# Scores of a second cross-attention from high and low halves in the round format, with keys kept in DRAM

## The chip, the cores and the metric

The kernel runs on one NeuronCore of a Trainium2 chip. The metric is the device time of one execution in microseconds; less is better. The core has TensorE (PE) for matmuls, VectorE (DVE), ScalarE (ACT) and GpSimd (POOL) for everything else, and SyncE (SP), which issues most of the DMAs here. The engines run their own instruction streams and meet only at semaphores.

## The reference, cut to what matters

Two layers of a perceiver-like network act on x (2 sequences of 64 tokens, 256 wide) with a context of 2 x 1024 rows of 512. Each layer is a cross-attention, a second mixing block and a mixture of eight experts. The change concerns the cross-attention of the second layer, in which each of 16 heads has 16 dimensions, the keys and values of the 1024 context rows are slices of the context itself, and those of the 64 tokens of the own sequence are projected:

```python
qkv = (x @ w_qkv.T).reshape(B, N, 3, H, D).transpose(2, 0, 3, 1, 4)
kv = context.reshape(B, N_c, 2, H, D).transpose(2, 0, 3, 1, 4)
k = jnp.concatenate([extra_k, k], axis=2)
attn = jnp.einsum('bhnd,bhmd->bhnm', q * scale, k)
attn = jax.nn.softmax(attn, axis=-1)
out = jnp.einsum('bhnm,bhmd->bhnd', attn, v)
return out @ w_proj.T + b_proj
```

## The kernel before

The program is written out engine by engine in one block; no planner orders it. It runs: first cross-attention, self-attention, first experts (units `f1b` to `f2e7`), second cross-attention, a state-space block with memory, second experts (`m1e0` to `m2e7`), store.

**Two number formats.** A matmul on plain float32 operands leaves two records per instruction in the trace. One whose operands have the type float32r (the round format) leaves one. For exactness a product in the round format is made from halves: `hi` is the value rounded to the format, `lo` is what is left, and a product of two split operands takes three matmuls (`TERMS`). The first cross-attention (`sim`, L1552; `attend`, L1596) and the experts (L1755, L1836) work so. The split halves of the context lie in `CXT` (turned, keys along the free axis) and `CXN` during the first cross-attention.

**Second cross-attention.** It is done in 16 rows of work, r = 0 to 15; row r is head pair j = r // 2 of sequence b = r % 2, with 128 query rows (2 heads x 64 tokens). For each r:

- `sim1(r)` (PE, L1890) makes 128 x 1024 scores in two plain float32 matmuls of 512 columns, one for each half `kh` of the keys. Each contracts over 32 partitions, and the two lie in different row groups of the array (`at = 64 * (j % 2) + 32 * kh`). `QZ` holds the queries, masked by head.
- DVE takes the maximum (L1244), and -max (L1254).
- ACT takes the exponential of the 1024 scores (L837) and of the 64 own scores (L841), which lie in `SELF`.
- `turn1(r - 2)` (PE, L1935) turns the 1152 probabilities in three groups c of three 128 x 128 transposes; ACT copies groups 0 and 2 out (L828), DVE group 1 (L1262).
- `attend1(r - 3)` (PE, L1953) multiplies them with the values, 9 matmuls in four column groups.

PE's order is sim1(r), turn1(r - 2), attend1(r - 3). `sim1(r)` waits for the exponential of row r - 2, whose scores used the same PSUM pair. Ahead of the loop PE projects the queries and the own keys (L1877, eight matmuls each, with weights that ACT laid out as `WDUP`, L800), makes sim1(0) and sim1(1), the own scores of both sequences for all pairs (`own_scores`, L1904), ten filler matmuls (`stay_warm`, L1475) and the own values (L1918). DVE adds `b_proj`, halves `D` and builds `hmask` just ahead of `QZ` (L1195 to L1201). `PV` collects the products and is copied out on DVE every four rows (L1230); `spread_sums` is L1217.

**POOL during this stage** splits the weights of `m1e0` and `m1e1` (four pieces of 1024 columns, L554 and L558), then splits bias rows (L609, L612) and scales a weight (L618). DVE's `spread_sums(0)` waits for the end of the bias rows, since both use `work`.

**Weights and the DMA queue.** Weights come in units of 1 MB, issued in a fixed order (`PLAN`) on SP's queue. A unit is loaded into a place once the unit that was there has been released. After the first cross-attention a cycle of NA + NB = 8 places is used (5 in `arena`, 3 in `ctxmem`); the other units of `ctxmem` hold `KEYS` (keys of the second cross-attention, 2 MB from the transposed context, L522) and `ctxN` (values, L523), which are loaded behind `f1e2`, and are filled with expert weights once the second cross-attention is through.

## Time and profile before

| | us |
|---|---|
| median of 3 runs | 467.27 (466.98 to 467.71) |
| the profiled execution | 467.19 |
| its span, first to last instruction | 465.4 |
| PE busy | 447.5 (96%) |
| DVE busy | 258.5 (56%) |
| ACT busy | 240.4 (52%) |
| POOL busy | 125.3 (27%) |

The span is what the trace shows; the profiled execution's own time is 1.8 us more. PE is busy for nearly all of the span, but its records are pipelined: a record of a matmul is longer than the step from one matmul to the next, so that steps between starts say more than durations. The granted TensorE clock is 1.0 over the whole span.

### The profile page before, as it was taken

How to read it: one execution, taken by the hardware profiler on the slowest of the kernel's cores; microseconds unless marked ns; L12 is line 12 of the kernel's file. 1: busy time of each engine (PE TensorE's matmuls, PEld its weight loads, DVE VectorE, ACT ScalarE, POOL GpSimd, SP SyncE). 2: the span in 40 equal slices, each digit the busy share in tenths (PEclk: the TensorE clock that was granted, in tenths of full speed). 3: DMA queues.
4: the chain of work that ended last, by engine and by line, in shares of the span. 5: the costliest groups of instructions: out<-in, count | busy, mean ns of one | idle time of the engine just before them, and what ended most of it. 6: DMA issues, size and time to landing. Idle time of an engine off the chain costs nothing.

```text
span 465.4 us, 8504 instructions
## 1 busy us (share of the span) xinstructions
PE 447.5 (96%) x3500; PEld 384.2 (83%) x3500; DVE 258.5 (56%) x455; ACT 240.4 (52%) x439; POOL 125.3 (27%) x113
## 2 busy tenths in 40 slices
PE   8999999999999999999987999999999999999997
PEld 7887989999897989999976677998666779778797
DVE  2656223245426233232045788978667765569996
ACT  2577334264445333252113778772888774347872
POOL 1120000002000500000021267988900000019795
PEclk9999999999999999999999999999999999999999
DMA  7925400005200020049990489891000039264000
GB/s 283 409 99 195 180 2 1 0 1 174 100 0 1 13 90 1 1 156 328 235 367 1 162 339 393 301 361 80 3 1 1 2 130 411 94 270 182 0 1 13
DMA packets 13191, 62.65 MB, mean 135 GB/s; under 512 B 1365, under 2 KB 3813, under 8 KB 7392
## 3 DMA queue, kind: packets, MB, share of 16 engines
q1 hardware_dynamic: 11072, 54.31, 31.7%
q0 software_dynamic: 2080, 7.80, 4.6%
q8 instruction: 28, 0.46, 0.4%
q14 instruction: 11, 0.09, 0.1%
HBM read 61.97 MB, written 0.13 MB: 133 GB/s over the span
## 4 chain that ended last, share of the span: by engine, by line
PE 78%; DVE 6%; ACT 6%; POOL 6%; issue 3%; DMA 1%; SPq 0%; DVEq 0%; ACTq 0%; POOLq 0%
PE W L1596 20%; PE W L1552 15%; PE W L1755 8%; POOL w_lo L558 5%; PE W L1836 4%; PE W L1890 4%; PE W L1935 3%; PE W L1569 3%; PE W L1953 2%; PE W L1618 2%; PE W L1475 2%; PE W L1856 1%; POOL small L567 1%; PE W L1877 1%; PE W L1659 1%
## 5 line engine op out<-in xcount | busy, mean ns | idle before, releaser
L1596 PE MATMUL W<-probs_turned_hi,ctx_split_hi 128*128 128x256 f32 x256 | 72.9, 285 | 2.5 <-issue 2.5
L1596 PE MATMUL W<-probs_turned_hi,ctx_split_lo 128*128 128x256 f32 x256 | 72.5, 283 | 0.0
L1596 PE MATMUL W<-probs_turned_lo,ctx_split_hi 128*128 128x256 f32 x256 | 72.4, 283 | 0.0
L1030 DVE TENSOR_TENSOR probs_turned_lo<-W,probs_turned_hi 128x512 fp32r<-128x512 f32 x32 | 20.6, 686 | 64.9 <-ACT probs_turned_hi L699 64.9
L1596 PEld LDWEIGHTS W<-probs_turned_hi,ctx_split_hi 128*128 128x128 f32 x256 | 49.1, 192 | 3.7 <-issue 3.3
L567 POOL TENSOR_TENSOR small<-small,const 128x1 f32<-128x1 f32 (+2 forms) x10 | 7.0, 699 | 164.5 <-DVE small L1103 75.3
L1596 PEld LDWEIGHTS W<-probs_turned_lo,ctx_split_hi 128*128 128x128 f32 x256 | 49.1, 192 | 0.2
L1596 PEld LDWEIGHTS W<-probs_turned_hi,ctx_split_lo 128*128 128x128 f32 x256 | 49.1, 192 | 0.0
L558 POOL TENSOR_TENSOR w_lo<-arena,w_hi 128x320 fp32r<-128x320 f32 x30 | 42.1, 1424 | 25.9 <-ACT w_hi L640 25.6
L718 ACT ACTIVATE pbuf<-W,small 128x1024 f32<-128x1024 f32 x16 | 17.9, 1117 | 59.5 <-DVE small L1050 59.5
L558 POOL TENSOR_TENSOR w_lo<-ctxmem,w_hi 128x320 fp32r<-128x320 f32 (+1 forms) x30 | 47.2, 1600 | 4.2 <-ACT w_hi L640 3.9
L993 DVE TENSOR_TENSOR w_lo<-arena,w_hi 128x704 fp32r<-128x704 f32 (+1 forms) x34 | 43.2, 1304 | 5.8 <-ACT w_hi L640 5.4
L1836 PE MATMUL W<-w_hi,acts 128*128 128x256 f32 x240 | 44.2, 286 | 0.0
L1552 PE MATMUL W<-ctx_turned_hi,q_keys_hi 128*128 128x512 f32 x128 | 41.1, 402 | 0.5 <-DVE q_keys_lo L1023 0.5
L640 ACT CAST w_hi<-arena 128x1024 fp32r<-128x1024 f32 x34 | 35.5, 1049 | 8.5 <-PE W L1755 4.1
L1552 PE MATMUL W<-ctx_turned_lo,q_keys_hi 128*128 128x512 f32 x128 | 39.7, 391 | 0.0
L1552 PE MATMUL W<-ctx_turned_hi,q_keys_lo 128*128 128x512 f32 x128 | 39.5, 390 | 0.0
L1836 PEld LDWEIGHTS W<-w_hi,acts 128*128 128x128 f32 x240 | 38.3, 191 | 0.1
L710 ACT COPY scr<-W 128x256 f32<-128x256 f32 x32 | 11.8, 368 | 48.9 <-PE W L1596 48.9
L993 DVE TENSOR_TENSOR w_lo<-ctxmem,w_hi 128x704 fp32r<-128x704 f32 x26 | 33.8, 1341 | 2.0 <-ACT w_hi L640 1.6
L1836 PE MATMUL W<-w_lo,acts 128*128 128x256 f32 x120 | 33.9, 282 | 0.0
L1042 DVE TENSOR_REDUCE small<-W 128x1 f32<-128x1024 f32 x16 | 19.6, 1223 | 25.5 <-PE W L1552 25.5
(403 smaller groups left out, 921.9 us busy)
## 6 DMA issues: line engine op xcount, KB each, us to landing
arena<-units_dram SPq DMA_DIRECT2D x22, 1024.0 KB, 6.2
ctxmem<-units_dram SPq DMA_DIRECT2D x16, 1024.0 KB, 7.8
fixed<-units_dram SPq DMA_DIRECT2D x6, 1024.0 KB, 6.4
pbuf<-ctx_dram POOLq DMA_DIRECT2D x4, 512.0 KB, 6.3
ctxmem<-ctxT_dram SPq DMA_DIRECT2D x8, 256.0 KB, 14.1
ctxmem<-ctx_dram SPq DMA_DIRECT2D x2, 1024.0 KB, 18.6
scr<-ctx_dram POOLq DMA_DIRECT2D x3, 512.0 KB, 4.1
vecs<-vectors_dram POOLq DMA_DIRECT2D x1, 1040.0 KB, 7.6
```

The costliest lines, as they stand in the source:

```text
L558: pool.tensor_tensor(w_slot(1, p)[:, lo:hi], half_in(p)[:, lo:hi], f32(w_slot(0, p)[:, lo:hi]), ALU.subtract).then_inc(ev("lo_by_gpsimd"), 1)
L640: act.copy(w_slot(0, p), half_in(p)).then_inc(ev(hi_done(p)[0]), 1)
L718: act.activation(probs0[:, r % 2, :], W[r % 2][:, :], ACT.Exp, bias=negm[:, r:r + 1], accum_out=stat[:, r, 1:2]).then_inc(ev("exp_done"), 1)
L993: dve.tensor_tensor(w_slot(1, p)[:, lo:hi], half_in(p)[:, lo:hi], f32(w_slot(0, p)[:, lo:hi]), ALU.subtract).then_inc(ev("lo_by_vector"), 1)
L1030: dve.tensor_tensor(PT[1][at], bank(4 + c).rearrange("p (t m) -> p t m", t=4), f32(PT[0][at]), ALU.subtract).then_inc(ev("pl_sb"), 1)
L1042: step(dve.tensor_reduce(mx[:, r % 2:r % 2 + 1], W[r % 2][:, :], AX_X, ALU.max))
L1552: mm = pe.matmul(W[r % 2][:, kh * 512:(kh + 1) * 512], QP[a][:, c, j, :], CXT[z][:, c, kh * 512:(kh + 1) * 512], start=(c == 0 and n == 0) ...
L1569: mm = pe.transpose(bank(4 + c)[:, t * P:(t + 1) * P], probs0[:, r % 2, (4 * c + t) * P:(4 * c + t + 1) * P], ident)
L1596: mm = pe.matmul(ps, CXN[a][:, t, c * P:(c + 1) * P], PT[z][:, t, :], start=(t == 0 and n == 0), stop=(t == KEYT - 1 and n == 2))
L1755: mm = pe.matmul(bank(4 + hf), XS[a][:, e, k, :], w_slot(z, p)[:, hf * 512:(hf + 1) * 512], start=u == "m1e0" and k == 0 and n == 0, stop= ...
L1836: mm = pe.matmul(bank(n % (E + 1) % 4)[:, 0:DIM], UTS[a][:, t, :], w_slot(z, p)[:, (t % 4) * DIM:(t % 4 + 1) * DIM], start=(t == 0 and i = ...
L1890: mm = pe.matmul(W[r % 2][:, kh * 512:(kh + 1) * 512], QZ[at:at + 32, j // 2, b].rearrange("p h q -> p (h q)"), KEYS[at:at + 32, b, j // 2 ...
```

## The change

It rebuilds the score products of the second cross-attention in the round format.

- **Keys.** The key half of `CXT`, already split into hi and lo for the first cross-attention, is stored to a DRAM buffer `kept_keys` (4 MB in four DMAs on SP's queue), and loaded back later as `KS`, 4 MB in eight DMAs, with hi in partitions 64 kh to 64 kh + 31 and lo in the 32 behind.
- **Queries.** They are projected four times over (`WDUPQ`), so that each 32 dimensions of a pair stand in all four groups of 32 partitions, then masked and split: hi (`QSH`) for pairs 0 to 3 by ACT, for pairs 4 to 7 by POOL from a copy (`QRAW`) that DVE makes; lo (`QSL`) by DVE.
- **sim1(r)** becomes four matmuls of 512 columns in the round format, each over 64 partitions: q hi and q lo, each with both key halves. One matmul over 64 partitions adds q times key hi and q times key lo.
- **Own scores** take 4, 12 and 16 matmuls in the round format at three points (pair 0, pairs 1 to 3, and pairs 4 to 7 within the loop at r = 7), all into PSUM bank 5, which `turn1` uses too. `turn1(6)` waits for DVE to have copied them out.
- **Moved.** `b_proj` to r = 3 of the loop; `D`, `hmask` and two new small steps to r = 1 of the first cross-attention. DVE's wait for the bias rows moves from r = 12 to r = 7.
- **Places.** `KS` takes four units of `ctxmem` where `KEYS` took two, so the cycle of places has 6 instead of 8, and six instead of four units are filled behind the second cross-attention, four of them as soon as all scores are made.

The diff, cut to its core:

```diff
-NR, NA, NB, NC = 4, 5, 3, 4
...
+PARTS_OF = [(kh, part) for kh in range(2) for part in range(2)]
...
-        put(units[freed + n], NR + NA + NB + n, after="xat")
+        put(units[freed + n], NR + NA + NB + n)
+        plan[-1][2].append(("sim1_done" if n < 4 else "pv1_ps", ROWT))
...
+        kept = nc.dram_tensor("kept_keys", (B, 2, DIM, NCTX), F32, kind="Internal").ap()
...
-        KEYS = cut(ctxmem, 0, B, 4, NCTX // 2)
-        ctxN = cut(ctxmem, B * KT * NCTX, B, KEYT, DIM)
+        KS = cut(ctxsplit, 0, B, PAIRS, NCTX // 2)
+        ctxN = cut(ctxmem, 4 * UNIT, B, KEYT, DIM)
...
+            def store_keys(b):
+                sync.wait_ge(ev("ctx_lo"), 8 if b == 0 else 10)
+                for part in range(2):
+                    sync.dma_start(kept[b, part].rearrange("(c p) k -> p c k", p=P), f32(CXT[part][:, 0:KT, :]))\
+                        .then_inc(ev("keys_kept"), 16)
             for n in range(3, len(PLAN)):
                 load(n)
+                if PLAN[n][0] == "wv1":
+                    store_keys(0)
+                if PLAN[n][0] == "att":
+                    store_keys(1)
...
+                    sync.wait_ge(ev("keys_kept"), 2 * B * 16)
                     for b in range(B):
-                        for jp, kh in ROWS_OF:
-                            at = 64 * jp + 32 * kh
-                            src = ctxT_in[b, 0:DIM, kh * 512:(kh + 1) * 512].rearrange("(m j p) k -> j p m k", j=2, p=32)
-                            sync.dma_start(KEYS[at:at + 32, b], src[jp]).then_inc(ev("ctxT_in"), 16)
+                        for kh, part in PARTS_OF:
+                            at = 64 * kh + 32 * part
+                            src = kept[b, part, :, kh * 512:(kh + 1) * 512].rearrange("(j p) k -> p j k", p=32)
+                            sync.dma_start(f32(KS[at:at + 32, b]), src).then_inc(ev("keys_in"), 16)
+                if PLAN[n][0] == f"f1e{NA + NB - 2}":
+                    for b in range(B):
                         sync.dma_start(ctxN[:, b], ctx_in[b, :, DIM:].rearrange("(t p) c -> p t c", p=P))\
                             .then_inc(ev("ctxN_in"), 16)
...
+                    pool.wait_ge(ev("q1_raw"), 1)
+                    for h in range(2):
+                        pool.tensor_tensor(QSH[:, 4:8, :, h, :], QRAW.rearrange("p j (b q) -> p j b q", b=B),
+                                           bc(hmask[:, h:h + 1].to_broadcast([P, B * NQ]), 1, 4)
+                                           .rearrange("p j (b q) -> p j b q", b=B), ALU.mult)\
+                            .then_inc(ev("q1_late_hi"), 1)
...
                     act.wait_ge(ev("sim_done"), TURN)
+                    act.wait_ge(ev("keys_kept"), 2 * 16)
...
-                w = unit("xat")[:, k * 768:k * 768 + 512].rearrange("p (j d) -> p j d", d=32)
-                ins = act.copy(WDUP[:, k].rearrange("p n m (j u d) -> p (n m j) u d", j=2, u=2), bc(w, 2, 2))
+                wq1, wk1 = [unit("xat")[:, k * 768 + n * DIM:k * 768 + (n + 1) * DIM] for n in range(2)]
+                act.copy(WDUPQ[:, k].rearrange("p j (u d) -> p j u d", u=4),
+                         bc(wq1.rearrange("p (j d) -> p j d", d=32), 2, 4))
+                ins = act.copy(WDUPK[:, k].rearrange("p m (j u d) -> p (m j) u d", j=2, u=2),
+                               bc(wk1.rearrange("p (j d) -> p j d", d=32), 2, 2))
...
+            def keep_masked_q(js, raw):
+                for h in range(2):
+                    act.mul(QSH[:, js, :, h, :], raw.rearrange("p j (b q) -> p j b q", b=B), hmask[:, h:h + 1])\
+                        .then_inc(ev("q1_hi"), 1)
+            act.wait_ge(ev("hmask_ready"), 1)
+            act.wait_ge(ev("q1_ps"), 1)
+            keep_masked_q(slice(0, 1), bank(6)[:, 0:P].rearrange("p (j t) -> p j t", j=1))
             act.wait_ge(*made("k1_ps"))
-            act.copy(K1, bank(7).rearrange("p (m t) -> p m t", m=4)).then_inc(*tick("k1_sb"))
-            def keep_own(b, jp):
-                if jp == 1:
-                    act.wait_ge(ev("self_ps"), b + 1)
-                else:
-                    act.wait_ge(ev("own_max"), b + 1)
-                act.copy(SELF[:, b].rearrange("p (m j) q -> p m j q", j=2)[:, :, jp, :],
-                         bank(SELF_BANK[b][jp])[:, 0:4 * NQ].rearrange("p (m q) -> p m q", m=4)).then_inc(ev("self_sb"), 1)
-            for b, jp in ((0, 1), (0, 0), (1, 1)):
-                keep_own(b, jp)
-            act.wait_ge(ev("self_sb"), 2)
+            act.copy(KS1, bank(5).rearrange("p (m t) -> p m t", m=4)).then_inc(*tick("k1_hi"))
+            act.wait_ge(*made("v1_ps"))
+            act.copy(vsb[:, :], bank(4)[:, 0:DIM]).then_inc(ev("v_sb"), 1)
+            act.wait_ge(ev("own_ps"), 1)
+            act.copy(scr[:, 5888:6016], bank(5)[:, 0:P]).then_inc(ev("self_sb"), 1)
+            act.wait_ge(ev("q1_ps"), 2)
+            keep_masked_q(slice(1, 4), bank(6)[:, P:].rearrange("p (j t) -> p j t", j=3))
...
+                if r == 1:
+                    dve.wait_ge(ev("cols_in"), 16)
+                    step(dve.tensor_scalar(p_("D"), p_("D"), 0.5, None, ALU.mult))
+                    step(dve.tensor_reduce(hmask, c_("hmask").rearrange("p (g h) -> p h g", h=2), AX_X, ALU.add))
+                    halves = c_("hmask").rearrange("p (a n) -> p a n", a=2)[:, :, 2:4]
+                    step(dve.tensor_tensor(minus_lo2, halves[:, 0], halves[:, 1], ALU.add))
+                    step(dve.tensor_reduce(minus_lo, minus_lo2, AX_X, ALU.add))
+                    dve.tensor_scalar(minus_lo, minus_lo, -4.0, None, ALU.mult).then_inc(ev("hmask_ready"), 1)
...
-            step(dve.tensor_tensor(x[:, :], x[:, :], v_("b_proj"), ALU.add))
-            step(dve.tensor_scalar(p_("D"), p_("D"), 0.5, None, ALU.mult))
-            step(dve.tensor_reduce(hmask, c_("hmask").rearrange("p (g h) -> p h g", h=2), AX_X, ALU.add))
-            dve.wait_ge(*made("q1_ps"))
-            for b in range(B):
-                q = bank(5).rearrange("p (m t) -> p m t", m=4)[:, :, b * NQ:(b + 1) * NQ]
-                dve.tensor_tensor(QZ[:, :, b], bc(q, 2, 2), bc(bc(hmask, 1, 4), 3, NQ), ALU.mult)\
-                    .then_inc(ev("qz_ready"), 1)
+            def keep_masked_q_lo(part, js, raw):
+                dve.wait_ge(*((ev("q1_hi"), 2 * part + 2) if part < 2 else (ev("q1_late_hi"), 2)))
+                for h in range(2):
+                    lows = QSL[0][:, js] if part < 2 else QSL[1]
+                    dve.scalar_tensor_tensor(out=lows[:, :, :, h, :], in0=raw.rearrange("p j (b q) -> p j b q", b=B),
+                                             scalar=hmask[:, h:h + 1], in1=f32(QSH[:, js, :, h, :]), op0=ALU.mult,
+                                             op1=ALU.subtract).then_inc(ev("q1_lo"), 1)
+            keep_masked_q_lo(0, slice(0, 1), bank(6)[:, 0:P].rearrange("p (j t) -> p j t", j=1))
+            dve.wait_ge(*made("k1_hi"))
+            dve.scalar_tensor_tensor(out=KS1, in0=f32(KS1), scalar=minus_lo, in1=bank(5).rearrange("p (m t) -> p m t", m=4),
+                                     op0=ALU.mult, op1=ALU.add).then_inc(*tick("k1_lo"))
...
+                    if r == 2:
+                        dve.wait_ge(ev("self_sb"), 2)
+                        dve.tensor_reduce(ownmax[:, 2:4], scr[:, 6016:6144].rearrange("p (r q) -> p r q", q=NQ),
+                                          AX_X, ALU.max)
+                        ins = dve.tensor_reduce(ownmax[:, 4:8], hn.rearrange("p (r q) -> p r q", q=NQ), AX_X, ALU.max)
...
+                if r == 1:
+                    keep_masked_q_lo(1, slice(1, 4), bank(6)[:, P:].rearrange("p (j t) -> p j t", j=3))
+                    dve.wait_ge(ev("q1_ps"), 3)
+                    dve.tensor_copy(QRAW, bank(7).rearrange("p (j t) -> p j t", j=4)).then_inc(ev("q1_raw"), 1)
...
+                if r == 3:
+                    step(dve.tensor_tensor(x[:, :], x[:, :], v_("b_proj"), ALU.add))
+                if r == 6:
+                    keep_masked_q_lo(2, slice(4, 8), QRAW)
+                if r == 7:
+                    dve.wait_ge(ev("rows2_split"), 2)
+                    dve.wait_ge(ev("own_ps"), 3)
+                    step(dve.tensor_copy(work[:, 512:], bank(5)))
+                    dve.tensor_reduce(ownmax[:, 8:], work[:, 512:].rearrange("p (r q) -> p r q", q=NQ), AX_X, ALU.max)\
+                        .then_inc(ev("own_late"), 1)
...
+            def query_rows(js, bk, first):
+                for j in js:
                     for k in range(KT):
-                        mm = pe.matmul(bank(bk)[:, m * P:(m + 1) * P], WDUP[:, k, n, m, :], xT[:, k, :],
+                        mm = pe.matmul(bank(bk)[:, (j - first) * P:(j - first + 1) * P], WDUPQ[:, k, j, :], xT[:, k, :],
                                        start=(k == 0), stop=(k == KT - 1))
-                mm.then_inc(*tick(("q1_ps", "k1_ps")[n]))
+                mm.then_inc(ev("q1_ps"), 1)
...
             def sim1(r):
                 b, j = r % 2, r // 2
-                if r < 2:
-                    pe.wait_ge(ev("qz_ready"), r + 1)
+                if r == 0:
+                    pe.wait_ge(ev("q1_lo"), 2)
                 if r >= 2:
                     pe.wait_ge(ev("exp1_done"), r - 1)
-                for kh in range(2):
-                    at = 64 * (j % 2) + 32 * kh
-                    mm = pe.matmul(W[r % 2][:, kh * 512:(kh + 1) * 512],
-                                   QZ[at:at + 32, j // 2, b].rearrange("p h q -> p (h q)"),
-                                   KEYS[at:at + 32, b, j // 2, :], start=True, stop=True)
+                for n, q in enumerate((QSH[:, j], QSL[j // 4][:, j % 4])):
+                    for kh in range(2):
+                        rows = slice(64 * kh, 64 * kh + 64)
+                        mm = pe.matmul(W[r % 2][:, kh * 512:(kh + 1) * 512], q[rows, b].rearrange("p h q -> p (h q)"),
+                                       KS[rows, b, j, :], start=(n == 0), stop=(n == 1))
                 mm.then_inc(ev("sim1_done"), 1)
...
+            even_done = [0]
+            def own_scores(js):
+                for jp in range(2):
+                    rows = slice(64 * jp, 64 * jp + 64)
+                    of_rows = [j for j in js if j % 2 == jp]
+                    if jp == 1 and of_rows:
+                        even_done[0] += 1
+                        mm.then_inc(ev("own_even"), 1)
+                        pe.wait_ge(ev("own_even"), even_done[0])
+                    for r in [2 * j + b for j in of_rows for b in range(B)]:
+                        b, j = r % 2, r // 2
+                        for n, q in enumerate((QSH[:, j], QSL[j // 4][:, j % 4])):
+                            mm = pe.matmul(bank(5)[:, (r % 8) * NQ:(r % 8 + 1) * NQ], q[rows, b].rearrange("p h q -> p (h q)"),
+                                           KS1[rows, j // 2, b * NQ:(b + 1) * NQ], start=(n == 0), stop=(n == 1))
+                mm.then_inc(ev("own_ps"), 1)
+            query_rows(range(1), 6, 0)
+            for m in range(4):
+                for k in range(KT):
+                    mm = pe.matmul(bank(5)[:, m * P:(m + 1) * P], WDUPK[:, k, m, :], xT[:, k, :],
+                                   start=(k == 0), stop=(k == KT - 1))
+            mm.then_inc(*tick("k1_ps"))
+            pe.wait_ge(ev("keys_in"), 16 * B * len(PARTS_OF))
             pe.wait_ge(ev("ctxN_in"), 16 * B)
-            def own_scores(b):
-                pe.wait_ge(ev("qz_ready"), B)
-                for j in range(PAIRS):
-                    m, at = j // 2, 64 * (j % 2)
-                    mm = pe.matmul(bank(SELF_BANK[b][j % 2])[:, m * NQ:(m + 1) * NQ],
-                                   QZ[at:at + 32, m, b].rearrange("p h q -> p (h q)"),
-                                   K1[at:at + 32, m, b * NQ:(b + 1) * NQ], start=True, stop=True)
-                mm.then_inc(ev("self_ps"), 1)
             sim1(0)
-            pe.wait_ge(*made("k1_sb"))
-            own_scores(0)
             sim1(1)
-            own_scores(1)
-            pe.wait_ge(ev("self_sb"), 2)
-            stay_warm(4, 5)
             for k in range(KT):
                 mm = pe.matmul(bank(4)[:, 0:DIM], xT[:, k, :], wx[:, k, 512:768], start=(k == 0), stop=(k == KT - 1))
             mm.then_inc(*tick("v1_ps"))
+            pe.wait_ge(*made("k1_lo"))
+            own_scores((0,))
+            query_rows(range(1, 4), 6, 0)
+            query_rows(range(4, 8), 7, 4)
+            pe.wait_ge(ev("self_sb"), 1)
+            pe.wait_ge(ev("q1_lo"), 4)
+            own_scores((1, 2, 3))
...
-                        pe.wait_ge(ev("self_sb"), 4)
+                        pe.wait_ge(ev("self_sb"), 2)
+                    elif c == 2:
+                        pe.wait_ge(ev("q1_raw"), 1)
+                    if r == 6 and c == 1:
+                        pe.wait_ge(ev("own_late"), 1)
...
+                if r == 7:
+                    pe.wait_ge(ev("pt1_sbV"), 6)
+                    pe.wait_ge(ev("q1_lo"), 6)
+                    own_scores((4, 5, 6, 7))
```

## Rows read from the trace of the kernel before

**Rows 1.** The page: each engine's busy time, its share and instructions.

```profile
PE 447.5 (96%) x3500; PEld 384.2 (83%) x3500; DVE 258.5 (56%) x455; ACT 240.4 (52%) x439; POOL 125.3 (27%) x113
```

**Rows 2.** Chain of waits, second cross-attention: start us, us, engine, tile, line.

```profile
332.44 1.06 PE W L1890 x4
...
362.07 1.06 PE W L1890 x4
363.13 1.13 PE W L1935 x9
...
365.04 1.08 PE W L1890 x4
```

**Rows 3.** Chain of waits: other products, for their steps.

```profile
19.24 1.99 PE W L1529 x32
...
60.07 5.48 PE W L1552 x24
...
317.58 3.84 PE W L1877 x32
```

**Rows 4.** PE's groups by shape: records, busy us, mean ns, idle before.

```profile
L1890 PE MATMUL W<-ctxmem,scr 32*128 32x512 f32 x64 | 18.2, 639 | 0.0
...
L1904 PE MATMUL W<-scr 32*128 32x64 f32 x32 | 2.5, 271 | 0.0
```

**Rows 5.** Timeline of PE: the own scores of the second sequence.

```profile
324.06 1.00 PE L1904 MATMUL W<-scr 32*128 32x64 f32 x14
```

**Rows 6.** Timeline of DVE, row 12: start us, us, idle before in brackets.

```profile
357.26 1.22 DVE L1244 TENSOR_REDUCE small<-W 128x1 f32<-128x1024 f32 x1 [1.03 <-PE W L1890]
358.51 0.21 DVE L1254 TENSOR_SCALAR small<-small 128x1 f32<-128x1 f32 x1
358.64 0.55 DVE L1262 COPY scr<-W 128x384 f32<-128x384 f32 x1
359.11 0.68 DVE L1217 TENSOR_TENSOR work<-small,const 128x512 f32<-128x512 f32 x1
```

**Rows 7.** Timeline of ACT: two rows early in the loop, without idle time between.

```profile
329.24 0.86 ACT L828 COPY scr<-W 128x384 f32<-128x384 f32 x2
329.97 1.15 ACT L837 ACTIVATE pbuf<-W,small 128x1024 f32<-128x1024 f32 x1
...
331.07 0.38 ACT L841 ACTIVATE pbuf<-scr,small 128x64 f32<-128x64 f32 x1
...
331.41 0.88 ACT L828 COPY scr<-W 128x384 f32<-128x384 f32 x2
```

**Rows 8.** Timeline of DVE ahead of the loop.

```profile
316.55 1.25 DVE L1195 TENSOR_TENSOR x<-x,vecs 128x256 f32<-128x256 f32 x1
317.83 2.21 DVE L1196 TENSOR_SCALAR cols<-cols 128x4 f32<-128x4 f32 x1
...
320.26 1.29 DVE L1201 TENSOR_TENSOR scr<-W,small 128x512 f32<-128x512 f32 x2
```

**Rows 9.** Timeline of POOL in the same stage.

```profile
317.60 2.41 POOL L558 TENSOR_TENSOR w_lo<-ctxmem,w_hi 128x1024 fp32r<-128x1024 f32 x1
...
330.20 2.12 POOL L609 CAST bias_rows<-work 8x1024 fp32r<-8x1024 f32 x2
...
336.54 1.90 POOL L618 TENSOR_TENSOR arena<-arena,cols 128x1024 f32<-128x1024 f32 x1
```

**Rows 10.** Timeline of DVE in the first cross-attention, row 1.

```profile
35.68 0.29 DVE L1066 TENSOR_TENSOR hn<-const,small 128x128 f32<-128x128 f32 x1
37.14 1.29 DVE L1030 TENSOR_TENSOR probs_turned_lo<-W,probs_turned_hi 128x512 fp32r<-128x512 f32 x2 [1.17 <-ACT probs_turned_hi L699]
```

**Rows 11.** Timeline of SP's DMA issues in the first experts.

```profile
261.63 12.50 SPq L494 DMA_DIRECT2D arena<-units_dram  x5
```

**Rows 12.** Timeline of ACT there: the two halves of `f1e5`, rounded.

```profile
269.63 1.99 ACT L640 CAST w_hi<-ctxmem 128x1024 fp32r<-128x1024 f32 x2
```

**Rows 13.** The page, DMA issues: KB each, median us from issue to landing.

```profile
arena<-units_dram SPq DMA_DIRECT2D x22, 1024.0 KB, 6.2
```

66 lines of the change are left out of this document (33 added, 33 removed).

## The prediction

> **What bounds the kernel now.** I read the page first: PE is busy for 96% of the span, no other engine for more than 56% [rows 1]. So a change can gain only where PE's own work shrinks or where PE waits. Then the chain of waits over the second cross-attention: it stays on PE from the first rows of the loop to the last, each row of work being scores (L1890), transposes (L1935) and products with the values (L1953) in turn [rows 2]. From sim1(4) at 332.44 to sim1(15) at 365.04 lie 11 steps of 2.96 us: 1.06 for the scores (362.07 to 363.13) and 1.91 for the rest (363.13 to 365.04). The timelines of the two engines that feed PE show how far they are from being the bound. DVE's row takes 1.85 us from its maximum to where the next thing starts (357.26 to 359.11), and it had waited 1.03 us for PE before [rows 6]. ACT's row takes 2.17 us when nothing holds it up (329.24 to 331.41) [rows 7]. So a PE step may shrink to about 2.2 us before ACT ends it.
>
> **The scores, what is gained.** Two plain float32 matmuls of 512 columns in two row groups take 1.06 us. How long four in the round format take, the trace does not show; I bound it. In the round format over the whole array a product of 512 columns steps at 5.48 / 24 = 0.228 us [rows 3]. Plain float32 over the whole array takes 3.84 / 16 = 0.24 us for 128 columns, so 0.96 for 512, and two in different row groups took 1.06 instead of 1.92: they overlap, at a cost of 0.10. That groups of 64 partitions overlap too is seen in L1529: 16 matmuls of 128 columns in 1.99 us, 0.124 each against 0.24 [rows 3]. Whether they do in the round format, no row shows. Bounds for sim1: below, two pairs that overlap for nothing, 2 x 0.228 = 0.46; above, four in line and the old overhead, 0.91 + 0.11 = 1.02. Scaled from 1.06 by half the streaming it is 0.53; with the whole 0.10 kept for each pair it is 0.63 (0.43 of streaming and 0.20). The nearest rows are these two, and I take 0.58. A PE step is then 1.91 + 0.58 = 2.49 us, above ACT's 2.17. Over rows 4 to 15 that is 12 x (1.06 - 0.58) = 5.8 us gained.
>
> The Trainium skill (TensorE: Matmul & The Clock Gate, Part 3: Packing small matmuls) lets a pack of row tiles take one matmul's time plus about 4 ns for each further tile, which would make sim1 0.46 us. The trace does not quite agree, with 0.10 us over one product's 0.96; by the rule the sum below would be 1.5 us better, by the row it stands.
>
> **Ahead of the loop.** I walked the three engines from PE's first projection (317.58) by these durations. On the kernel before the same walk puts sim1(4) at 332.44 and sim1(15) at 365.00, where the trace has 332.44 and 365.04, so I trust it to a few tenths. After the change: pair 0's queries 0.48 and own keys 1.92 end at 319.98. By then its hi halves (ACT, two short steps) and lo halves (DVE, two more) are there, since `b_proj`, `D` and `hmask`, which now hold DVE until 320.26 [rows 8], are gone from the spot. sim1(0) and sim1(1) take 1.16 instead of two 1.06, the own values follow, then pair 0's own scores and 14 more projections at 0.24 (3.36 us). In PE's work, 24 projections (5.76 us) stand where 16 stood (3.84) [rows 3], 16 own products of one record where there were 32 records (2.5 us busy) [rows 4], and the filler matmuls are gone: what sim1 and the filler give, the projections mostly take. sim1(2) starts near 326.9, turn1(0) is held a little by the second batch of own scores that ACT copies, and sim1(4) starts at 331.6: 0.8 us gained.
>
> **Inside the loop, what is given back.** At r = 6 DVE makes the lo halves of pairs 4 to 7, twice 512 columns, at 0.65 each by L1201 (1.29 for two) [rows 8], and at r = 7 it has the copy to `PV` besides. A DVE row of 1.85 us has 0.64 of slack in a step of 2.49, so 1.3 + 0.6 us do not fit. Moreover these lo halves read only SBUF, and where DVE did so next to POOL it stood: L1196, four columns wide, took 2.21 us and ended at 320.04, with POOL's L558 beside it (320.01) [rows 8, 9]. POOL reaches its L618 of 1.90 us near 338.9 (330.2, then two masks of 512 columns at half of L558's 2.41, then 6.3 us for the bias rows as before, 330.20 to 336.54), just when DVE starts at 339.4: up to 1.2 us more. What is late next: attend1(4) waits for `PV`'s copy (PE idle 1.4), the third batch of own scores waits for DVE's copy of turn1(5) (1.1), the batch runs, and turn1(6)'s second group waits until DVE has copied it and taken its maximum (0.5). The batch: 16 products of 64 columns. The nearest rows are the old own scores, 14 records in 1.00 us, some 0.065 each [rows 5]; so 1.04, plus 0.2 for the wait between even and odd pairs, 1.24 in all. At half of that cost per product the sum is 0.9 us better, at 0.12 each 1.8 us worse. Together 1.4 + 1.1 + 1.2 + 0.5 = 4.2 us lost with POOL in the way, 3.0 without.
>
> **The rest, costed at nothing.** Five small DVE steps at row 1 of the first cross-attention, some 0.2 each: DVE stood idle for 1.17 us right behind them [rows 10]; without that cover they cost 1.0. The copies to DRAM (4 MB) go on SP's queue behind `wv1` and `att`; what stands behind them there is not wanted before the scores end, and ACT's added wait for the first store is met by then, since a store of 2 MB is two units' worth of time. POOL's two masks, 2.4 us, delay the bias rows to 338.9, while DVE asks for them at r = 7, after 344. `b_proj` at r = 3 falls in DVE's slack. ACT's layout of the weights grows by half, by 1 us, while PE is still on the last unit of the first experts. Six places instead of eight: `f1e5` now goes where `f1b` was, so it is issued at 261.6 instead of before; its halves are rounded at 269.63, 8.0 us later, and a unit lands in 6.2 [rows 11, 12, 13]. Later units keep the same distance of six units, each of which PE takes more than 2.7 us for (twelve steps of 0.228), so they have 10 us and more. Without this cover each late unit costs its lateness, once.
>
> **Sum.** -5.8 - 0.8 + 4.2 = -2.4; the walk as a whole gives -2.3 with POOL in the way and -3.4 without. I keep -2.3. Against the profiled execution (467.19) that is 464.9; the median of the runs shown lies 0.08 higher, and I say 465.0. A tenth of a microsecond in sim1 moves this by 1.2.
>
> **The rivals.** (a) Full overlap: sim1 at 0.46. For it speaks that the 0.10 may belong to the plain format's two records; against it that a pair of 512 columns shows it. 463.5, and 462.4 if POOL is not in the way either. Chance 0.13. (b) Slower, by one mechanism: round-format matmuls in two row groups do not overlap. Place: L1890's four matmuls; price: sim1 at 0.91 to 1.02, which gives +2.0 to +3.4, 469.2 to 470.7. It decides from sim1 = 0.77 us up, where the gain is gone. For it speaks only that no row shows the format in row groups; against it L1529 and L1890. 0.13. (c) The gain is eaten: the third batch costs 0.12 per product, or DVE gets to it later still, and what the loop gains goes into r = 6 to 8. -0.5 to +0.5, 467. 0.14. (d) A unit arrives late in the first experts with six places. Little margin only at `f1e5` (1.8 us); some 468 to 469. 0.06. The forecast, 463.8 to 466.2, has 0.52; the last 0.02 I leave to what I have not thought of.
>
> **How the numbers follow.** A change within 0.2% (0.93 us) cannot be told from none. Faster is the forecast and (a), and a little of (c), 0.67; the same is most of (c), 0.12; slower is (b), (d) and a part of (c), 0.21. The range reaches from (a) to the near end of (b), 462.6 to 469.0.
>
> **What would show it.** Right: L1890 steps of 0.5 to 0.65 us in the chain, a loop step near 2.5, ACT and DVE not the releasers of PE but for r = 6 to 8, where PE idles 2 to 3 us before the third batch. Wrong: L1890 steps of 0.9 or more; PE waiting for ACT's exponentials in every row; a gap at L1755 or L1836 in the first experts, released by a DMA; DVE late at row 1 of the first cross-attention.

## The result, and the profile after

The changed kernel takes 471.0 us (median of 4 executions, 470.7 to 471.4) against 467.2 (467.0 to 467.7) before. The ratio is 1.0062, 95% interval 1.0039 to 1.0084: slower. By the ratio that is 2.9 us, by the two medians 3.8. Ratios leave out executions in a slower state; here and below that is one, of the kernel before without its filler. I had forecast 465.0 with a range up to 469.0. The profiled execution took 471.41 with a span of 469.6, before 467.19 and 465.4 [rows 1].

The page, the span, the engines' busy time, and the row of the granted clock in 40 slices:

```profile
span 469.6 us, 8537 instructions
...
PE 449.0 (96%) x3506; PEld 389.6 (83%) x3506; DVE 259.3 (55%) x465; ACT 242.4 (52%) x444; POOL 127.4 (27%) x115
...
PEclk9999999999999999999999999999888999999999
```

The granted clock was 1.0 over the whole span before. Now three slices of the second cross-attention stand lower. By stretches (window, us and busy PE with its records, granted clock, DMA share):

```profile
326.00:329.00 3.00, 2.31 (x19) 0.95 0.00 0
329.00:332.00 3.00, 3.00 (x13) 0.50 0.00 0
332.00:335.00 3.00, 3.00 (x36) 0.99 0.00 0
...
345.00:350.00 5.00, 3.36 (x25) 0.92 0.00 0
350.00:353.00 3.00, 3.00 (x26) 0.50 0.02 5
353.00:356.00 3.00, 3.00 (x15) 0.50 0.00 0
356.00:366.00 10.00, 10.00 (x124) 1.00 0.01 2
```

Two stretches ran at 0.50, the lower of the clock's two levels (1.2 instead of 2.4 GHz), and each follows a few microseconds in which PE was not full. The chain of waits, from row 7 of the loop on, answers to [rows 2]:

```profile
345.39 0.56 DVE scr L1323
345.99 1.09 PE W L1980 x8
...
348.30 0.70 DVE work L1332
349.03 0.70 DVE small L1333
349.86 1.51 PE W L2027 x6
351.38 1.42 PE W L2045 x18
352.80 1.15 PE W L1962 x3
353.95 2.11 PE W L2027 x9
356.06 0.77 PE W L2045 x18
356.83 0.67 PE W L1962 x4
357.50 1.14 PE W L2027 x9
```

Read it from below. A plain row is 0.67 for the scores (L1962), 1.14 for the transposes and 0.77 for the products: 2.57 us from one sim1 to the next, where it was 2.96. So the main part of the change works: the four matmuls in the round format overlap in their two row groups. At half clock the same transposes take 2.11 and the same products 1.42. Above stand the own scores (L1980), released by DVE, and DVE's copy and maximum of them, which release the next transposes. PE's waits in this stage, as the list of waits has them (us in total, times, longest):

```profile
PE W L1980 <- DVE scr L1323: 0.9, 1, 0.9
PE W L2027 <- DVE small L1333: 0.6, 1, 0.6
PE W L1980 <- DVE acts L1251: 0.6, 1, 0.6
...
PE W L2045 <- DVE ctxmem L1286: 0.4, 1, 0.4
```

**How I measure below.** The stages ahead of this one scatter: PE's first projection starts at 317.3 to 318.2 us in most of the traces and at 319.0 to 319.6 in three. The kernel before scatters too: its medians beside the experiments are 468.7 to 469.0, its lowest 466.9. Its mean granted clock was 0.993 or 0.996 in 28 of these 92 executions, so a mean just below full doesn't tell in which stage a fall lies. So beside each time I give the *stage*: from PE's first projection to the start of sim1(15), from the profiled execution. Before it is 47.4 us (317.58 to 364.97), after 51.9 (317.69 to 369.61). My forecast comes to 45.6 by the same measure: 14.0 to sim1(4), 11 steps of 2.49, 4.2 lost at r = 6 to 8. So there are 6.3 us to explain.

### The profile page after: what moved, and what is told of

It is laid out like the page before. It is cut to its first block, busy times and chain, and to the rows that moved or that the text cites. A ratio compares the mean times of both kernels' runs of the same rounds, so it can differ in the third digit from the quotient of the medians.

```text
span 469.6 us, 8537 instructions
## 1 busy us (share of the span) xinstructions
PE 449.0 (96%) x3506; PEld 389.6 (83%) x3506; DVE 259.3 (55%) x465; ACT 242.4 (52%) x444; POOL 127.4 (27%) x115
## 4 chain that ended last, share of the span: by engine, by line
PE 75%; DVE 8%; ACT 6%; POOL 5%; issue 3%; DMA 1%; SPq 0%; DVEq 0%; ACTq 0%; POOLq 0%
PE W L1665 20%; PE W L1621 15%; PE W L1824 8%; POOL w_lo L589 5%; PE W L1905 4%; PE W L2027 3%; PE W L1638 3%; PE W L1962 2%; PE W L2045 2%; PE W L1687 2%; DMA fixed<-units_dram 1%; PE W L1544 1%; DVE small L1300 1%; PE W L1925 1%; PE W L1980 1%
## 5 line engine op out<-in xcount | busy, mean ns | idle before, releaser
L589 POOL TENSOR_TENSOR w_lo<-arena,w_hi 128x320 fp32r<-128x320 f32 (+1 forms) x38 | 56.5, 1511 | 19.2 <-ACT w_hi L677 18.9
L1035 DVE TENSOR_TENSOR w_lo<-arena,w_hi 128x704 fp32r<-128x704 f32 (+1 forms) x40 | 49.1, 1256 | 6.3 <-ACT w_hi L677 5.8
L677 ACT CAST w_hi<-arena 128x1024 fp32r<-128x1024 f32 x40 | 41.7, 1049 | 13.3 <-PE W L1905 6.9
L589 POOL TENSOR_TENSOR w_lo<-ctxmem,w_hi 128x320 fp32r<-128x320 f32 (+1 forms) x22 | 32.8, 1510 | 10.9 <-ACT w_hi L677 10.6
L1824 PE MATMUL W<-w_hi,acts 128*128 128x512 f32 x104 | 33.5, 398 | 0.1
```

What stands on the lines that cost most here:

```text
L589: pool.tensor_tensor(w_slot(1, p)[:, lo:hi], half_in(p)[:, lo:hi], f32(w_slot(0, p)[:, lo:hi]), ALU.subtract).then_inc(ev("lo_by_gpsimd"), 1)
L677: act.copy(w_slot(0, p), half_in(p)).then_inc(ev(hi_done(p)[0]), 1)
L1035: dve.tensor_tensor(w_slot(1, p)[:, lo:hi], half_in(p)[:, lo:hi], f32(w_slot(0, p)[:, lo:hi]), ALU.subtract).then_inc(ev("lo_by_vector"), 1)
L1824: mm = pe.matmul(bank(4 + hf), XS[a][:, e, k, :], w_slot(z, p)[:, hf * 512:(hf + 1) * 512], start=u == "m1e0" and k == 0 and n == 0, stop= ...
```

## Experiment: is it the clock?

First theory (C): PE's waits, which filler matmuls had covered before, let the clock fall, and the fall costs what is missing. Filler goes into three waits of the changed kernel. (A filler matmul is plain float32 and leaves two records; what I called ten filler matmuls in the kernel before are five, with ten records.)

```diff
+            pe.wait_ge(ev("v_sb"), 2)
+            stay_warm(4, 6)
             pe.wait_ge(ev("self_sb"), 1)
             pe.wait_ge(ev("q1_lo"), 4)
             own_scores((1, 2, 3))
...
+                        pe.wait_ge(ev("exp1_done"), 8)
+                        stay_warm(2, 5)
                         pe.wait_ge(ev("own_late"), 1)
...
+                    pe.wait_ge(ev("exp1_done"), 7)
+                    stay_warm(0, 8)
                     pe.wait_ge(ev("pt1_sbV"), 6)
```

All three places:

> The changed kernel with PE's idle time filled in three places: 6 filler matmuls ahead of the second batch of own scores, 8 ahead of the third batch at r = 7, 5 ahead of turn1(6)'s second group. Nothing else differs. Theory C (clock): the two stretches at half the granted clock behind PE's waits cost 1.7 and 3.4 us, so with PE kept at work the clock stays full, turn1 and attend1 keep 1.13 and 0.77 us to the end, and the time is 466 to 467. Rival W (waits): the batches of own scores and the waits around them cost the time, the clock falls behind them in work that has slack; then the filler takes up idle time alone or adds to it, 471 to 472.

The first alone:

> The changed kernel with filler ahead of the second batch of own scores only. Theory C: the first stretch at half clock (near 329 to 332 us) is gone, the second stays, 1.7 us less, 469.3. Rival W: no gain, 471. A third way: the first fall only moves the next one, so that the second comes at another place; then 469 to 472, with the clock row telling where.

The two in the loop alone:

> The changed kernel with the two fillers at r = 7 and in turn1(6) only. Theory C: the stretch near 350 to 356 us is gone, the first stays, 3.4 us less, 467.6. Rival W: 471 to 472.

And the kernel before without its own filler:

> The kernel before without its filler matmuls in front of the own values. Nothing of the change is in it. Theory C: if it is the missing filler that lets the clock fall, it falls here too, behind the wait for the own scores' copies, and costs 1.5 to 2 us, 468.7 to 469.2. Rival: the filler was only time spent (about 1.2 us), then 466.0 to 467.3 with the granted clock at full.

| | median (range), us | ratio to before | stage |
|---|---|---|---|
| all three | 471.9 (469.8 to 473.4) | 1.0068 (1.0043 to 1.0093) | 50.0 |
| ahead | 472.1 (470.7 to 472.3) | 1.0070 (1.0044 to 1.0097) | 51.0 |
| in the loop | 470.5 (468.9 to 473.9) | 1.0063 (1.0037 to 1.0089) | 50.4 |
| before, no filler | 468.4 (467.2 to 474.7) | 1.0017 (0.9977 to 1.0057) | 47.1 |

Theory C fell in this form. The filler did move the clock in the profiled executions: ahead alone, the first fall was gone and the second stayed; in the loop alone, the second was gone and the first stayed. But the time did not come down by what I expected. With all three the clock was 1.0 in the profiled execution, and the stage came down by only 1.9 us. The trace says why. Eight fillers kept PE until 346.24, two microseconds after attend1(4) had ended at 344.25; the wait that they filled had lasted 0.94. They covered the wait and lengthened it: from attend1(4) to the first product it took 1.0 us more. The kernel before without its filler gave two answers. In 7 of 10 executions the clock stayed at 1.0, the profiled one among them, and the stage was 0.3 shorter. In the other 3 the mean clock was 0.982 and the span 7 us longer (472.3 to 472.9 against 465.4); none of the 22 executions of the kernel before beside them was like that. Where they lost it I can't say, since no trace of them is at hand. So a missing filler does not by itself make the clock fall, but may let it.

So a clean price of the clock was still missing. The changed kernel, run again beside others, gave a first one:

> The changed kernel itself, once more beside the others on the same chip, so that they can be compared with it directly. 471 us, with the two stretches at half clock near 329 to 332 and 350 to 356 us. If they come and go between executions, the theory that they follow from what PE does there needs a bound.

It took 470.4 (468.2 to 472.6; ratio 1.0038, 1.0017 to 1.0059). None of its 10 executions had a full clock (a mean of 0.999 or 1.0; they had 0.989 to 0.996), nor had any of the first four (0.989). The profiled one had only the second fall, and its stage was 50.4. The same program falls once or twice. The kernel before had a mean below that in 8 of the 28 executions beside it, so the falls are not the change's alone, but with it they came every time. Last, fillers no longer than the waits (2, 3 and 2 instead of 6, 8 and 5):

> The changed kernel with filler matmuls no longer than PE's waits: 2, 3 and 2 instead of 6, 8 and 5 in the same three places. From PE's first projection to sim1(15) the changed kernel took 51.9 us with two half-clock stretches, 50.4 with one, the kernel with long fillers 50.0. Theory C (the clock costs some 3.5 us, the long fillers gave 2 of them back): 48.0 to 48.5, with the granted clock full throughout. Rival (short fillers leave too much idle time, the clock falls all the same): 50 to 52. Either way it shows what the change costs at full clock against the 47.5 us of the kernel before.

Measured: 469.2 (467.5 to 470.7), ratio 1.0017 (0.9998 to 1.0037), stage 48.0, as forecast by theory C in this second form (48.0 to 48.5). The clock by stretches, same columns as above:

```profile
329.00:332.00 3.00, 2.76 (x19) 1.00 0.00 0
...
345.00:350.00 5.00, 4.84 (x49) 1.00 0.01 3
350.00:353.00 3.00, 3.00 (x43) 1.00 0.00 0
353.00:356.00 3.00, 3.00 (x35) 1.00 0.00 0
```

What follows: two falls cost 51.9 - 48.0 = 3.9 us. 1.0 of it lies ahead of sim1(4), 2.9 between sim1(7) and sim1(10). In the repeated run the second fall alone cost 50.4 - 48.0 = 2.4, so these prices move by half a microsecond with where the fall lies. At full clock the change is 0.6 us longer in this stage than the kernel before, and gives 0.4 back in sim1(15) itself: no gain, no loss (span 465.7 against 465.4). The filler is no sure cure: 5 of 10 executions still had a mean clock of 0.996 or less, four of them 0.993 or less. Of the 23 of the kernel before beside them 10 had 0.996 or less, two of them 0.993.

## Experiment: what does the third batch of own scores cost?

> The changed kernel without the third batch of own scores: the 16 products of pairs 4 to 7, PE's waits before them, DVE's copy and maximum of them and the wait in turn1(6) are left out; rows 8 to 15 use the own scores of rows 0 to 7 instead. It tells what the batch costs with all that hangs on it. From the start of sim1(7) to that of sim1(9) the changed kernel takes 10.71 us, two plain steps 5.14. Theory N (the batch and its waits are the larger part of the loss, the clock comes on top): 5.1 to 5.5 us for these two steps, no half clock behind them, 464 to 465. Rival K (DVE's low halves and the copy to PV are what holds PE, and they are still there): 6.5 us or more for the two steps, 466 or more.

Measured: 465.5 (464.0 to 467.1), ratio 0.9934 (0.9909 to 0.9959), stage 45.3. From sim1(7) to sim1(9) it takes 5.54 us instead of 10.71, and no half clock follows, though the first fall (329 to 332) was there. The kernel leaves work out, so it is a probe and no version to use. Theory N holds, with both numbers just above its ranges (5.1 to 5.5, 464 to 465): the batch with all that hangs on it costs 6.6 us of the stage, 5.2 in these two steps and 1.5 in the slow step behind them. DVE's low halves and the copy to `PV`, still there, cost 0.4. Rival K fell.

What the batch is made of shows in PE's timeline of the changed kernel (start, duration, idle before in brackets):

```profile
344.67 0.38 PE L2045 MATMUL W<-scr,vsb 128*32 128x128 f32 x2
345.99 0.29 PE L1980 MATMUL W<-acts 64*128 64x64 f32 x1 [0.94 <-DVE scr L1323]
346.12 0.27 PE L1980 MATMUL W<-acts,ctxsplit 64*128 64x64 f32 x1
...
346.79 0.27 PE L1980 MATMUL W<-acts,ctxsplit 64*128 64x64 f32 x1
347.12 0.29 PE L1980 MATMUL W<-acts 64*128 64x64 f32 x1
...
347.93 0.27 PE L1980 MATMUL W<-acts,ctxsplit 64*128 64x64 f32 x1
...
348.68 0.55 PE L2027 MATMUL W<-const,pbuf 128*128 128x128 f32 x3
349.86 1.51 PE L2027 MATMUL W<-const,pbuf 128*128 128x128 f32 x6 [0.64 <-DVE small L1333]
```

A product starts every 0.11 us, not every 0.065, with a break of 0.33 between the even and the odd pairs, where PE waits for itself.

## Experiment: one bank or two

The kernel before had the own scores of even and odd pairs in two PSUM banks and issued them in turn [rows 5]. The changed one has them all in bank 5, first the even pairs, then, after a wait, the odd ones.

```diff
-                for jp in range(2):
-                    rows = slice(64 * jp, 64 * jp + 64)
-                    of_rows = [j for j in js if j % 2 == jp]
-                    if jp == 1 and of_rows:
-                        even_done[0] += 1
-                        mm.then_inc(ev("own_even"), 1)
-                        pe.wait_ge(ev("own_even"), even_done[0])
+                evens, odds = [[(j, b) for j in js if j % 2 == jp for b in range(B)] for jp in range(2)]
+                for at in range(max(len(evens), len(odds))):
+                    both = [side[at:at + 1] for side in (odds, evens)]
...
-                            mm = pe.matmul(bank(5)[:, (r % 8) * NQ:(r % 8 + 1) * NQ], q[rows, b]...
+                            rows, bk = slice(64 * (j % 2), 64 * (j % 2) + 64), odd_bank if j % 2 else 5
...
-                    step(dve.tensor_copy(work[:, 512:], bank(5)))
+                    dve.tensor_copy(halves[0][:, :, 0], halves[1][:, :, 0]).then_inc(ev("own_late"), 1)
+                    dve.tensor_copy(halves[0][:, :, 1], halves[2][:, :, 1]).then_inc(ev("own_late"), 1)
```

> The changed kernel with the own scores of odd pairs in a second PSUM bank (6 in the second batch, 7 in the third), so that products of even and odd pairs alternate and can run beside each other in the two row groups. In the changed kernel one product takes 0.113 us in line; the kernel before had them in two banks, 0.07 each. Theory: the same overlap holds in the round format, a product comes down to 0.06 to 0.07 us, the third batch from 1.9 to about 1.0 us and the second by about 0.5; as DVE's copies are split too, turn1(6) is let go a little earlier: 1.3 to 2 us less, 469 to 469.8. Rival: a product takes 0.113 by itself, alternating or not: 471.

And the same banks and copies with the products in the old order, even pairs first, without the wait between:

> The kernel with own scores in two banks, but its products in the changed kernel's order: all of the even pairs, then all of the odd ones. Banks, copies and the early release of the banks are as in the two-bank kernel (profiled span 463.4). It tells the alternation from the rest. Theory (overlap of the two row groups): a product takes 0.11 us again, the second batch 1.3 and the third 1.8 us, 1.4 us more in all at full clock: 464.8 to 465.5 of span, and if the clock falls in the longer thin stretch, up to 468. Rival (the gain came from the second bank and the early release alone): as the two-bank kernel, 463.4 to 463.8 of span.

Two banks: 466.6 (465.2 to 468.4), ratio 0.9959 (0.9931 to 0.9987), stage 45.7, clock full in 4 of 5 executions. This edit (second bank, products in turn, split copies, no wait between) gives 6.2 us of the stage and makes the changed kernel faster than the one before. I had expected 469 to 469.8: I had not put in that the clock would stay full. In turn, pairs of records start together; PE's timeline of the third batch:

```profile
344.40 0.30 PE L1982 MATMUL W<-acts 64*128 64x64 f32 x2 [0.98 <-issue]
344.50 0.31 PE L1982 MATMUL W<-acts,ctxsplit 64*128 64x64 f32 x2
...
345.17 0.31 PE L1982 MATMUL W<-acts,ctxsplit 64*128 64x64 f32 x2
345.28 0.51 PE L1967 MATMUL W<-ctxsplit,acts 64*128 64x512 f32 x2
...
345.94 1.20 PE L2035 MATMUL W<-const,pbuf 128*128 128x128 f32 x9
```

Even pairs first, same two banks:

```profile
344.42 0.27 PE L1983 MATMUL W<-acts 64*128 64x64 f32 x1 [0.98 <-issue]
...
344.86 0.30 PE L1983 MATMUL W<-acts 64*128 64x64 f32 x2
...
345.67 0.27 PE L1983 MATMUL W<-acts,ctxsplit 64*128 64x64 f32 x1
...
346.42 1.65 PE L2036 MATMUL W<-const,pbuf 128*128 128x128 f32 x9
```

From the first product to the transposes behind sim1(8): 2.69 us in one bank, 2.00 in two, 1.54 in two and in turn. My expectation for the even-first kernel was only half right: without the wait the odd pairs start beside the even ones by themselves, after four records. So in these traces the alternation is worth 0.5, the second bank with no wait 0.7, and the split copies took away the 0.64 behind them. The even-first kernel took 467.2 (465.2 to 468.9; 0.9975, 0.9954 to 0.9997), stage 47.5, but most of its 1.8 us over the other is again a half-clock stretch (347 to 350 at 0.50): 1.3 if the alternation is worth 0.5. Its two executions at full clock have the spans of the two-bank kernel (463.4 and 463.5 against 463.4), which is what the rival said. So the 0.5 stands in one pair of traces and does not show in the spans; what the second bank and the copies give does (465.7 with the fitting fillers in one bank).

Of the 6.2 us, 1.7 lie ahead of sim1(4), 3.2 between sim1(7) and sim1(9) and 1.3 in the step behind. By the price above 3.9 of it are the clock, and 2.3 are products and waits. The Trainium skill (TensorEngine Tiling (Array Packing), Gotcha 1: PSUM Pressure) says that different row tiles can't access the same PSUM bank at once, and the wait between even and odd pairs guards against that. No run here has both groups at work in one bank; they did overlap wherever the banks differ, in the changed kernel too, where sim1(8) starts at 347.60 beside the last odd products.

## Experiment: DVE's low halves, and POOL

I had feared that DVE's low halves of pairs 4 to 7 would stand beside POOL at r = 6. After the change they didn't (1.41 us for two, DVE at 342.08, POOL done at 340.71). To take them from the full row, one each went to r = 4 and 5:

```diff
-                if r == 6:
-                    keep_masked_q_lo(2, slice(4, 8), QRAW)
+                if r in (4, 5):
+                    keep_masked_q_lo(2, slice(4, 8), QRAW, (r - 4,))
```

> The changed kernel with DVE's two low halves of pairs 4 to 7 made at r = 4 and r = 5, one each, instead of both at r = 6. Theory: PE's waits of 0.35 us before attend1(4) and 0.94 us before the third batch go, since each of the two fits DVE's slack of about 0.6 us in a row; that is 1.2 us at full clock, and up to 2.8 more if the clock then stays full: 467 to 470. Rival: the half clock and the batch stay as they are and the low halves delay rows 4 to 6 as much as they did row 7; 471.

Measured: 470.6 (470.0 to 472.1), ratio 1.0051 (1.0033 to 1.0069), stage 50.5, with two half-clock stretches (330 to 333 and 350 to 353): the rival. The two took 0.87 and 1.81; the second stood beside POOL's step of 1.90 us (339.31 to 341.21). Then all edits together, with a new order ahead of the loop:

> The whole computation, with all three edits and a new order ahead of the loop: low halves spread over r = 4 and 5; own scores in two banks, the bank released by DVE's copies rather than by its maximum; the query rows of pairs 1 to 3 projected before the own values, their halves made before the first row's own maximum, and the second batch copied by DVE instead of ACT. No filler matmul is added. If the waits and the batch cost what the trace of the changed kernel shows (2.7 us of a late sim1(4), 1.9 us of waits and 0.9 of products at r = 7 and 8) and the clock falls only behind them, sim1(4) starts near 331.8, the loop's steps are 2.57 but for 1.1 us once, and the time is 462 to 464, below the kernel before. If the half clock comes back all the same, 464 to 467. If the reorder makes ACT or DVE late in rows 0 to 3, sim1(4) stays near 333 to 334, 464 to 466.

Measured: 468.5 (466.5 to 469.3), ratio 0.9988 (0.9972 to 1.0004), stage 47.4, above all three of my ranges. sim1(4) started at 331.75, as forecast, at full clock. Then PE waited 1.09 us in row 6 and 1.24 in row 7 for DVE, and from sim1(6) to sim1(8) it took 9.70 us, where the two-bank kernel takes 7.52. DVE there:

```profile
334.80 2.49 DVE L1247 SCALAR_TENSOR_TENSOR ctxsplit<-ctxmem,small,acts 128x512 fp32r<-128x512 f32 x1
...
339.06 2.26 DVE L1247 SCALAR_TENSOR_TENSOR ctxsplit<-ctxmem,small,acts 128x512 fp32r<-128x512 f32 x1
```

and POOL:

```profile
334.37 2.37 POOL L649 TENSOR_TENSOR bias_rows<-work,bias_rows 8x1024 fp32r<-8x1024 f32 x1
...
338.87 1.90 POOL L655 TENSOR_TENSOR arena<-arena,cols 128x1024 f32<-128x1024 f32 x1
```

Each low half ends 0.55 us after the POOL instruction beside it, whatever its start. I read that as standing until POOL was done (336.74, 340.77) and then running. With POOL idle it takes 0.7 (1.41 for two). The changed kernel's low halves of pairs 1 to 3, which read the raw values from PSUM, run at their own pace (0.57 each) in the middle of a POOL instruction of 2.36 us (324.53 to 326.89):

```profile
324.53 2.36 POOL L589 TENSOR_TENSOR w_lo<-ctxmem,w_hi 128x1024 fp32r<-128x1024 f32 x1
...
325.59 1.14 DVE L1251 SCALAR_TENSOR_TENSOR acts<-W,small,acts 128x384 fp32r<-128x384 f32 x2 [0.41 <-ACT acts L849]
```

The Trainium skill (SBUF — State Buffer, Who interferes with whom) has it so: a DVE instruction with two SBUF inputs contends with a GpSimd one that reads SBUF, the ports that they share are locked by one of them at a time, and a DVE instruction with at most one SBUF input stays clear. These rows agree.

With the low halves back at r = 6 and the rest kept:

> The two-bank kernel with the new order ahead of the loop, and DVE's low halves left at r = 6. sim1(4) starts at 331.8 as in the kernel with all edits. But then r = 6 comes before POOL's last step ends (340.8), and DVE's first low half should stand beside it. Theory (a DVE step that reads both operands from SBUF stands while POOL works on SBUF): its first low half takes 1.2 to 2 us instead of 0.70, and the 0.9 us won at the head are lost again at r = 7: span 463.0 to 463.8. Rival (no such contention): 0.70 for each low half, span 462.5.

Measured: 466.6 (465.0 to 468.5), ratio 0.9956 (0.9933 to 0.9980), stage 45.9: 0.5 won ahead of sim1(4) (I had said 0.9), 0.65 lost at r = 7, since the two low halves take 2.10 beside POOL instead of 1.41. The theory holds; its span of 463.0 to 463.8 is met only without the 1.3 us by which this execution's stage began late (318.99). Three fillers in its wait at r = 7:

> The two-bank kernel with the new order ahead of the loop and 3 filler matmuls in PE's wait before the third batch. The filler is not longer than the wait and costs nothing: 45.3 to 45.9 us from PE's first projection to sim1(15), as without it (45.85), and the clock stays full in more of the executions, so that the median comes down by up to 1 us. If the clock follows from something else, the granted clocks scatter as before.

466.8 (465.2 to 467.4), 0.9959 (0.9943 to 0.9975), stage 45.9; 8 of 10 executions at full clock against 4 of 7. Too few to settle it.

## Experiment: a version below both

So the low halves must not read SBUF twice. ACT makes the high halves of pairs 4 to 7 at the head instead of POOL, DVE the low ones from PSUM:

```diff
+                    if r == 0:
+                        act.wait_ge(ev("q1_ps"), 3)
+                        keep_masked_q(slice(4, 8), bank(7).rearrange("p (j t) -> p j t", j=4))
```

> The whole computation: own scores in two banks alternating; the new order ahead of the loop; and pairs 4 to 7 made high and low right there, the high halves by ACT behind row 0's exponential and the low halves by DVE from PSUM, instead of by POOL and DVE from SBUF. No low half is left in the loop, nothing of it runs beside POOL's work on SBUF. If the loop then has no wait at r = 7 (0.35 and 0.94 us before) and the head costs at most 1 us more than in the kernel with all edits (sim1(4) at 331.75), sim1(4) starts near 332.5, and the span is 461.5 to 462.5, the time 463.3 to 464.3. If ACT and DVE at the head are the bound, sim1(4) at 334, and the time near 465.

Measured: 466.9 (465.3 to 468.6), ratio 0.9967 (0.9948 to 0.9987), stage 46.2. I had expected 463.3 to 464.3. The waits at r = 7 are gone (0.18 left), but turn1(0) waits 1.07 for the low halves, and a half-clock stretch follows (332 to 335). With banks 6 and 7 exchanged, so that only attend1(0) needs them:

> The whole computation. As the kernel in which ACT makes the high halves of pairs 4 to 7 and DVE the low ones from PSUM at the head, with banks 6 and 7 exchanged for the raw queries, so that the low halves have to be there by attend1(0) and not by turn1(0)'s third group; ACT's part comes behind row 1's exponential instead of row 0's, and the step on b_proj is at r = 12. If the head then costs 12.6 to 12.8 us from sim1(0) to sim1(4) (12.0 without these halves, 12.5 in the two-bank kernel, 14.3 in the ACT kernel, half clock in it) and no wait is left at r = 7, it takes 44.6 us from PE's first projection to sim1(15), 1.1 less than the two-bank kernel: 464.2 where the stages ahead are undisturbed, a ratio to the kernel before of about 0.993. If a half-clock stretch comes, 1.5 us more.

Measured: 463.9 (463.7 to 466.1), ratio 0.9916, interval 0.9893 to 0.9938, stage 44.5 (44.6 forecast), clock full in 4 of 6 executions. The timeline of PE in rows 6 and 7:

```profile
340.24 0.73 PE L1961 MATMUL W<-ctxsplit,acts 64*128 64x512 f32 x4
340.90 1.20 PE L2029 MATMUL W<-const,pbuf 128*128 128x128 f32 x9
...
343.05 0.30 PE L1976 MATMUL W<-acts 64*128 64x64 f32 x2 [0.17 <-issue]
...
344.61 1.20 PE L2029 MATMUL W<-const,pbuf 128*128 128x128 f32 x9
```

The wait of 0.94 is 0.17, the one of 0.64 is gone, and the batch with all around it costs 1.1 us (sim1(7) to sim1(8) 3.69 instead of 2.57). This kernel beats the one before by 3.3 us of span (462.1 against 465.4) and the changed one by 7.5.

## Why the prediction was wrong

Each step in terms of the stage, forecast 45.6, measured 51.9:

- **The clock: the step that failed, +3.9.** "the filler matmuls are gone: what sim1 and the filler give, the projections mostly take" and the waits at r = 6 to 8 were priced as time alone. I saw a granted clock of 1.0 over the whole span before and took every duration of it as fixed; yet my own walk had PE idle for 2 to 3 us there and filled the rest with narrow products. The term was not in the sum, nor in the range, nor a rival. It makes the difference between slower and the same: with fitting fillers the kernel runs as fast as the one before. It does not save the forecast of a gain, which the next two items used up.
- **Ahead of the loop, +1.6 at full clock** (15.6 us to sim1(4) instead of 14.0). The second batch costs 1.4 us where 12 products at 0.065 make 0.8, with a wait of 0.63 before it, for the low halves of pairs 1 to 3: I had ACT and DVE ready in time. The rest is the first four sim1, 0.3 together, and a wait of 0.24 in turn1(1) for DVE's copy.
- **sim1, +0.9.** 0.66 us against 0.58: within the bounds (0.46 to 1.02), nearer to the 0.63 that keeps the 0.10 of overlap cost for each pair. The 0.10 itself was read too small: 0.24 us for 128 columns is a stretch with its ends in it, while the records of L1877 start every 0.112 us, 0.22 for a matmul's two. So 512 columns make 0.89, and the plain pair costs 0.17 over it. Rivals (a) and (b) are both out by the 0.66; that the time came out next to (b)'s 469.2 to 470.7 is chance. (Its +2.0 to +3.4 should by my own 1.2 per tenth have been +1.7 to +3.0.) The loop step is 2.57 for 2.49.
- **r = 6 to 8, right in sum by luck, wrong in parts.** 4.2 forecast, 4.2 measured at full clock. But no part of it was POOL, for which I had put 1.2. The products took 1.9 instead of 1.24, since the row I took (0.065) [rows 5] was that of records, two to a product, alternating in two banks and row groups, and the change puts them in line in one bank. Within one group the records start every 0.11 us there too. I had priced the new order as 0.2 for one wait. Rival (c) named the price ("0.12 per product") and put the time at 467, with no clock in it either; its 1.8 us also counts more products than my 0.9 for half the cost does (28 of them at 0.055 more make 1.5). The waits took the rest: 0.35, 0.94 and 0.64.
- **What cost nothing, cost nothing.** The copies to DRAM, the five DVE steps, six places instead of eight, POOL's masks: the profile up to 317 us is the old one, shifted by 0.1. Rival (d) is out: with the stage starting 0.1 late, no unit can have cost more than that.
- POOL in the way: wrong for this kernel, since the loop ran 2.7 us later than forecast, and right as a mechanism. Where the loop was in time (the kernel with all edits, the one with the low halves back at r = 6), it struck.

**Open:** what exactly sets off the fall. It comes behind stretches of waits and narrow products, not behind one alone: the kernel before without its filler had a mean clock of 0.982 in 3 of 10 executions, the kernel without the third batch has the first fall and not the second, and of one program some executions fall and others don't. The Trainium skill (TensorE: Matmul & The Clock Gate, Part 1: The HAM clock gate) says that the hardware sets the clock by how busy PE has been, and that the point of the change varies from run to run; these runs agree, and tell no more.

## What to carry to other kernels

Where a change thins out PE's work, by waits or by narrow products, price it twice: as time, and as a stretch of half clock behind it (here 1.0 us for one of 3.4 us, 2.4 to 2.9 for one of 6.8), even where the profile before shows a full clock everywhere. A step time read from products that alternate between row groups and banks is not the price of the same products in line. And before moving a DVE step, see what POOL does there: with two SBUF inputs the step here waited out POOL's instruction (2.49 and 2.26 us instead of 0.70), with one in PSUM it didn't (0.57).

## What the runs showed of the hardware

Row groups of 64 partitions overlap in the round format: two pairs of 512 columns in 0.66 us, against 0.228 for one over the whole array [rows 3]; 0.10 per pair is overhead, and in plain float32 0.17 for a pair of matmuls, 0.09 for each pair of records. What it consists of no run here shows. Products of 64 columns follow each other at 0.11 us in one row group, the step at which the filler's records of 128 columns start, and two by two in two groups. Matmuls in different row groups and banks overlap even when they are issued group after group, from the fifth record on.
